# Ranks, rows and tables of the low nodes made under layer 1's first sums, and the plan for crowded nodes behind the last one-hot

## What is computed

```python
def _sage_conv(x, src, dst, Wl, Wr, b):
    agg = segment_sum(x[src], dst)            # 3125 rows
    deg = segment_sum(ones_like(dst), dst)
    mean = agg / maximum(deg, 1.0)[:, None]
    return mean @ Wl + x @ Wr + b
h = relu(conv1(h)); h = relu(conv2(h)); h = relu(conv3(h)); out = x + conv4(h)
```

## Time and profile before

| | |
|---|---|
| median of 3 runs | 645.88 us (645.56 to 646.54) |
| the profiled execution | 645.63 us, of it 643.8 us in the span of the trace |
| TensorE busy | 615.5 us (96%) |
| VectorE, ScalarE, GpSimd busy | 318.9, 194.1, 41.8 us |
| mean granted clock of TensorE | 0.986 of full speed |
| first fill, degrees, first round | TensorE's first step starts at 15.47 us, its degrees at 50.60, its first sum at 53.84; the degrees' last turn of the round at 103.29 |

### The profile page before, as it was taken

The page is one execution under the profiler, slowest core; times in us unless marked ns, Lnnn a source line. Parts: engine busy times, 40 slices in busy tenths (PEclk is TensorE's granted clock), DMA queues, the critical chain, the costliest instruction groups (busy, mean ns, idle before and its releaser), DMA issues.

```text
span 643.8 us, 10273 instructions
## 1 busy us (share of the span) xinstructions
PE 615.5 (96%) x4155; PEld 339.3 (53%) x4156; DVE 318.9 (50%) x616; ACT 194.1 (30%) x411; POOL 41.8 (6%) x91
## 2 busy tenths in 40 slices
PE   5678999999999999999999999999999999999998
PEld 4435555656555555554444445444445646556586
DVE  6977876878888779721211111111126343334421
ACT  3876866365653622300111001122122010000100
POOL 8001300000000000000000000000002020110110
PEclk9977999999999999999999999999999999999999
DMA  8401200510210202142433531534451133030330
GB/s 265 104 1 46 85 1 3 184 57 6 68 53 15 88 23 83 34 139 67 147 89 89 151 86 50 106 98 111 140 126 33 43 86 113 2 115 10 105 116 33
DMA packets 59687, 51.00 MB, mean 79 GB/s; under 512 B 31670, under 2 KB 44507, under 8 KB 59640
## 3 DMA queue, kind: packets, MB, share of 16 engines
q1 hardware_dynamic: 59284, 49.74, 26.8%
q0 software_dynamic: 240, 0.37, 0.2%
q10 hardware_dynamic: 116, 0.24, 0.1%
HBM read 28.15 MB, written 16.60 MB: 70 GB/s over the span
## 4 chain that ended last, share of the span: by engine, by line
PE 86%; DVE 6%; ACT 3%; DMA 2%; issue 2%; POOL 1%; SPq 0%; DVEq 0%; ACTq 0%; POOLq 0%
PE agg_ps L2362 34%; PE window_ps L2362 19%; PE lin_ps L2297 5%; PE window_ps L2183 5%; PE lin_ps L2246 3%; PE lin_ps L2140 2%; PE agg_ps L2338 2%; PE lin_ps L2266 2%; PE lin_ps L2305 2%; DVE early L1479 1%; PE lin_ps L2384 1%; PE degree_ps L2061 1%; PE turn_ps L2183 1%; PE window_ps L2338 1%; ACT counts L1876 1%
## 5 line engine op out<-in xcount | busy, mean ns | idle before, releaser
L2362 PE MATMUL agg_ps<-counts,H 128*128 128x512 f16 (+2 forms) x1026 | 235.1, 355 | 1.0 <-DVE aggT L1570 0.8
L2362 PEld LDWEIGHTS agg_ps<-counts,H 128*128 128x128 f16 (+1 forms) x1026 | 79.2, 98 | 56.2 <-issue 10.2
L1876 ACT ACTIVATE counts<-window_ps 128x400 f16<-128x400 f32 x150 | 73.5, 506 | 62.8 <-PE window_ps L2183 49.7
L1472 DVE TENSOR_TENSOR counts<-early 128x2048 f16<-128x2048 bf16 x66 | 78.0, 1213 | 7.2 <-PE window_ps L2183 4.8
L2362 PE MATMUL window_ps<-counts,early 128*128 128x512 f16 (+2 forms) x346 | 77.8, 379 | 0.0
L2362 PEld LDWEIGHTS window_ps<-counts,early 128*128 128x128 f16 (+1 forms) x346 | 33.5, 98 | 41.3 <-issue 3.4
L2362 PE MATMUL window_ps<-counts,H 128*128 128x512 f16 (+1 forms) x291 | 55.2, 346 | 0.0
L2183 PEld LDWEIGHTS window_ps<-counts 128*128 128x128 f16 x412 | 30.9, 99 | 33.2 <-issue 4.6
L1472 DVE TENSOR_TENSOR early<-early 128x1024 f16<-128x1024 bf16 (+1 forms) x69 | 43.9, 684 | 7.6 <-PE window_ps L2183 6.1
L2362 PE MATMUL agg_ps<-counts,early 128*128 (+4 forms) x297 | 46.5, 314 | 0.0
L2183 PE MATMUL window_ps<-counts 128*128 128x100 f16 x412 | 41.4, 210 | 1.0 <-DVE counts L1472 0.8
(11 more groups left out here) (302 smaller groups left out, 712.5 us busy)
## 6 DMA issues: line engine op xcount, KB each, us to landing
selfT<-hT_d SPq DMA_DIRECT2D x18, 512.0 KB, 4.2
hT_d<-newT SPq DMA_DIRECT2D x12, 512.0 KB, 4.6
rdeg<-rdeg_d SPq DMA_DIRECT2D x22, 256.0 KB, 4.1
counts<-in_x_dram SPq DMA_DIRECT2D x6, 512.0 KB, 8.1
hT_d<-counts SPq DMA_DIRECT2D x6, 512.0 KB, 3.6
newH<-in_x_dram SPq DMA_DIRECT2D x6, 512.0 KB
out_dram<-newT SPq DMA_DIRECT2D x5, 512.0 KB
hT_d<-newT SPq DMA_DIRECT2D x6, 256.0 KB, 3.8
```

What stands on the lines that cost most here:

```text
L1472: v.tensor_tensor(hots_of(group).rearrange("p r a (n d) -> p r a n d", d=2), pairs.unsqueeze(1).unsqueeze(1).broadcast_to([P, n, 2, P // 2 ...
L1876: a.activation(counts[:, :, 2 * w * WIN:2 * (w + 1) * WIN].rearrange("p t (a w) -> p a t w", a=2), window_bank(FILL_AT[w])[:, 0:2 * KEYS]. ...
L2362: last = m((agg_ps, window_ps)[bank][:, h, 0:n], tile[:, part, h * P:(h + 1) * P], counts[0:rows_, k, chunk_cols(c, n)], start=first and p ...
```

## The change

The diff leaves every operation as it is and moves some. On VectorE the four parts of `below` leave the fill and stand at sums 2, 3, 4 and 5 of the first round; `plan_high` moves from before pair 30 of the fill to behind its last pair; both `bases_late` go to sum 9, `late_rows` to 11, `square_weights` to 8, the tables to 16 and 20. On ScalarE three of the four moments of chunk place 4 leave the middle of the fill (one goes to its end), `first_rows(3)` goes from the fill's end to sum 8, the moments of places 5 and 6 and the norms move. On TensorE `rank_low` goes from pair 28 of the fill to sum 7, `own_products(1)` and `load_heavy` behind the last pair, `turn_bases` to sum 10, the squares to 10, 11 and 13, `select_late` to 14 and 18, now with waits for `norms_made` of 3 and `first_rows_made`. The squares wait for three tables instead of five; the wait for five stands at sum 24.

VectorE (`between` of the fill, then `first_round`):

```diff
-                       12: lambda: (below(0), h0_low_part(0)), 17: lambda: h0_low_part(1), 18: lambda: h0_shift(2),
-                       19: lambda: edge_tables(), 25: lambda: below(1), 28: lambda: (below(2), below(3)),
-                       30: lambda: plan_high()}
+                       12: lambda: h0_low_part(0), 17: lambda: h0_low_part(1), 18: lambda: h0_shift(2),
+                       19: lambda: edge_tables()}
...
+            plan_high()
             load_heavy(dve, regs, 0)
...
-            first_round = {0: lambda: (h0_moments(3), bases_late(2)), 1: lambda: (degrees(0), h0_low_part(2)),
-                           3: lambda: bases_late(3), 5: lambda: (late_rows(), h0_shift(3)), 7: lambda: h0_shift(4),
-                           9: lambda: h0_low_part(3), 10: lambda: square_weights(), 11: lambda: late_tables(2),
-                           12: lambda: h0_low_part(4), 13: lambda: h0_shift(5), 15: lambda: h0_low_part(5),
-                           16: lambda: (late_tables(3), h0_shift(6)), 21: lambda: h0_low_part(6)}
+            first_round = {0: lambda: h0_moments(3), 1: lambda: (degrees(0), h0_low_part(2)), 2: lambda: below(0),
+                           3: lambda: below(1), 4: lambda: below(2), 5: lambda: (h0_shift(3), below(3)),
+                           7: lambda: h0_shift(4), 8: lambda: square_weights(), 9: lambda: (bases_late(2), bases_late(3)),
+                           10: lambda: h0_low_part(3), 11: lambda: late_rows(), 12: lambda: h0_low_part(4),
+                           13: lambda: h0_shift(5), 15: lambda: h0_low_part(5), 16: lambda: late_tables(2),
+                           17: lambda: h0_shift(6), 20: lambda: late_tables(3), 21: lambda: h0_low_part(6)}
```

ScalarE (`between`):

```diff
-                       21: lambda: h0_moment(4, 0), 24: lambda: h0_moment(4, 1),
-                       25: lambda: (h0_copy(1), h0_moment(4, 2)),
-                       26: lambda: (h0_moment(4, 3), h0_high_part(2), own_copy(1)),
-                       31: lambda: (first_rows(3, slice(0, MID), degree_ps[:, 0:MID]), h0_moment(5, 0), h0_moment(5, 1))}
+                       21: lambda: h0_moment(4, 0), 25: lambda: h0_copy(1), 26: lambda: h0_high_part(2),
+                       31: lambda: (own_copy(1), h0_moment(4, 1))}
```

ScalarE, the new `first_round`:

```diff
+            first_round = {0: lambda: (h0_root(3), h0_moment(4, 2)), 1: lambda: h0_moment(4, 3),
+                           2: lambda: (h0_root(4), h0_moment(5, 0)), 3: lambda: h0_moment(5, 1),
+                           4: lambda: h0_moment(5, 2), 5: lambda: h0_copy(2),
+                           6: lambda: (h0_high_part(3), h0_moment(5, 3)), 7: lambda: own_copy(2),
+                           8: lambda: (first_rows(3, slice(0, MID), degree_ps[:, 0:MID]), h0_high_part(4), h0_copy(3)),
+                           9: lambda: h0_moment(6, 0), 10: lambda: h0_moment(6, 1),
+                           11: lambda: (h0_root(5), own_copy(3), norms(0)), 12: lambda: (h0_moment(6, 2), norms(1)),
+                           13: lambda: (h0_high_part(5), h0_moment(6, 3), norms(2)),
+                           14: lambda: (h0_root(6), late_sources(2)), 15: lambda: h0_copy(4),
+                           16: lambda: (own_copy(4), spread_sources(2)), 17: lambda: h0_high_part(6),
+                           18: lambda: late_sources(3), 21: lambda: spread_sources(3), 24: lambda: copy_degrees(0)}
```

TensorE (`squares`, `select_late`, the two tables, the fill's loop):

```diff
-                pe.wait_ge(step_tables, 5)
+                pe.wait_ge(step_tables, 3)
...
-                pe.wait_ge(lo_made, 3)
+                pe.wait_ge(first_rows_made, 1)
+                pe.wait_ge(norms_made, 3)
...
-                       27: lambda: h0_turn(1), 28: lambda: (rank_low(), own_products(1))}
-            first_round = {3: lambda: turn_bases(), 4: lambda: h0_turn(2), 7: lambda: own_products(2),
-                           8: lambda: (h0_turn(3), select_late(2)), 11: lambda: own_products(3),
-                           13: lambda: select_late(3), 15: lambda: h0_turn(4), 16: lambda: own_products(4),
-                           17: lambda: squares(0), 19: lambda: squares(1), 21: lambda: squares(2),
-                           24: lambda: turn_degrees(0)}
+                       27: lambda: h0_turn(1)}
+            first_round = {4: lambda: h0_turn(2), 7: lambda: (rank_low(), own_products(2)),
+                           8: lambda: h0_turn(3), 10: lambda: (turn_bases(), squares(0)),
+                           11: lambda: (own_products(3), squares(1)), 13: lambda: squares(2),
+                           14: lambda: select_late(2), 15: lambda: h0_turn(4), 16: lambda: own_products(4),
+                           18: lambda: select_late(3), 24: lambda: (pe.wait_ge(step_tables, 5), turn_degrees(0))}
...
-                if i == len(FILLS[-1]) - 2:
-                    load_heavy(pe, regs, 0)
...
+            own_products(1)
+            load_heavy(pe, regs, 0)
             heavy_of(-1)
```

More of the change, by code:

```diff
@@ L1982, in late_sources @@
                 whole_sources(piece + 1, p1 - p0, whole_late)
-            first_round = {0: lambda: h0_root(3), 1: lambda: h0_moment(5, 2),
-                           3: lambda: (h0_root(4), h0_moment(5, 3)), 5: lambda: h0_copy(2),
-                           6: lambda: h0_high_part(3), 7: lambda: (h0_moment(6, 0), h0_moment(6, 1), own_copy(2)),
-                           8: lambda: (h0_high_part(4), h0_copy(3)), 9: lambda: late_sources(2),
-                           10: lambda: h0_moment(6, 2), 11: lambda: (spread_sources(2), h0_root(5), own_copy(3)),
-                           12: lambda: h0_moment(6, 3), 13: lambda: (h0_high_part(5), h0_root(6)),
-                           14: lambda: late_sources(3), 15: lambda: h0_copy(4), 16: lambda: own_copy(4),
-                           17: lambda: (norms(0), h0_high_part(6)), 18: lambda: norms(1),
-                           20: lambda: spread_sources(3), 21: lambda: norms(2), 24: lambda: copy_degrees(0)}
+            first_round = {0: lambda: (h0_root(3), h0_moment(4, 2)), 1: lambda: h0_moment(4, 3),
[9 more added lines that the diff above has]
+                           18: lambda: late_sources(3), 21: lambda: spread_sources(3), 24: lambda: copy_degrees(0)}
             second_round = {0: lambda: h0_copy(5), 2: lambda: (root_row(0), h0_copy(6)),
```

## The result

| | before | after |
|---|---|---|
| median of 4 runs | 646.21 us (645.56 to 647.79) | 660.26 us (659.62 to 660.57) |
| the profiled execution, its span | 645.63, 643.8 us | 660.32, 658.5 us |
| TensorE's first step | 15.47 us | 16.11 us |
| degrees, first sum | 50.60, 53.84 us | 44.65, 48.06 us |
| last degree turn of the round | 103.29 us | 117.73 us |

The ratio is 1.022 (95% interval 1.0199 to 1.024). The predicted 649.1 us had the sign and not the size: the time lies 8 us above the range. All of the difference arises ahead of the last degree turn: it comes 14.4 us later, and the rest is unchanged. Of the 14.4 us, 0.64 arise before the fill: TensorE's first step starts later in this execution, where both kernels run the same code. The page of the changed kernel (busy time, then tenths in 40 slices of the span) shows where the rest is.

What follows compares the result with a forecast made beforehand. TensorE was taken to bound the first round, and VectorE and ScalarE the fill. Terms -7.2 + 3.45 + 1.0 + 1.0 + 4.15 + 1.25 - 0.2 = +3.45 on 645.63 gave 649.1 us, own range 647 to 651.4, 8-in-10 range 645.0 to 652.0.

Steps and rivals of the forecast that it cites:

- fill, from there to the degrees: Fill: without comparisons and ranks, ScalarE's copies and VectorE's plan let the degrees start near 43.4 us, -7.2 us.
- ranks: TensorE in the first round: sixteen rank products of 512 columns, covered by nothing, +3.45 us.
- sum 5: Sums 0 to 5: VectorE's degrees and comparisons delay one-hots that TensorE needs, +1.0 us (0 to 2).
- bases at sum 9: Sum 9: first rows behind the own copy, then bases, make one-hots late for TensorE, +1.0 us (0.5 to 1.5).
- squares and selection: Sums 11 to 14: three TensorE waits for norms that ScalarE reaches late, 1.95, 0.95 and 1.25, +4.15 us (2 to 5).
- tables at sum 20: Sum 20: late tables need sources selected at sum 18, so one-hots come late, +1.25 us (0 to 2).
- before's own short waits: Two short waits of the kernel before go with the moved turn_bases and selections, -0.2 us.
- The third rival: TensorE's clock falls in the new waits around sums 10 to 14, costing 2.8 us more: 651.9 us; chance 0.10.
- ScalarE's chain: Fill on ScalarE: 9.0 us of work after own_products(0) ends near 33.4, so the last window is stored at 42.6 us.
- The first rival: First round: TensorE stays the only bound, norms and tables come in time, 641.9 us; chance 0.14.
- the second: First round: the norms' 1.95 us is real, most other waits take each other's place, 645 us; chance 0.16.

Runs made afterwards that it cites:

- experiment 3: Changed kernel with the low parts of chunks 3 and 6 moved ahead of the bases and late tables on VectorE: 651.99 us, ratio 1.0101 to the kernel before.
- experiment 2: Changed kernel with only the low part of chunk 6 moved ahead of the late tables at sum 20 on VectorE: 657.26 us, ratio 1.0176 to the kernel before.
- experiment 5: Changed kernel with only the first rows moved ahead of the own copy of chunk 2 on ScalarE at sum 7: 655.01 us, ratio 1.0138 to the kernel before.
- experiments 1: Changed kernel with only the low part of chunk 3 moved ahead of the bases, at sum 9 on VectorE: 654.52 us, ratio 1.0133 to the kernel before.
- experiment 4: Changed kernel with both low parts moved up and each of three norms first in its place on ScalarE: 648.71 us, ratio 1.0045 to the kernel before.
- experiment 7: The version of experiment 4 with the low nodes' comparisons back in VectorE's fill, ranks still at sum 7: 651.92 us, ratio 1.0074 to the kernel before.
- experiments 9: Experiment 4 plus the fill's end rearranged, first rows ahead of own copy 2, late selection, sources and tables earlier: 645.62 us, ratio 0.9989 to the kernel before.
- 10: Experiment 9 plus later VectorE shift and high part of chunk 3, and ScalarE's own copy 3 one window copy later: 645.57 us, ratio 0.9993 to the kernel before.
- 6: Kernel before with only the plan for crowded nodes moved behind the last one-hot: 649.2 us, ratio 1.0043 to the kernel before.
- experiment 11: Experiment 9 with chunk 3's shift and high part as in experiment 10, heavy counts released ahead of the plan's end: 643.38 us, ratio 0.9963 to the kernel before.

## Why the prediction was right or wrong

| term | predicted | changed kernel | with both low parts moved (3) |
|---|---|---|---|
| start of TensorE's first step | none | +0.64 | +0.02 |
| fill, from there to the degrees | -7.2 | -6.59 | -6.59 |
| ranks | +3.45 | +3.46 | +3.46 |
| sum 5 | +1.0 | +1.28 | +1.28 |
| low part of chunk 3 at sum 8 | none | +5.11, clock +1.6 | 0 |
| bases at sum 9 | +1.0 | (hidden by the wait at 8) | +1.20 |
| squares and selection | +4.15 | 1.82 + 1.11 + 0.83 = +3.76 | +3.75 |
| a window copy at 104.65 | none | +0.74 | +0.74 |
| tables at sum 20 | +1.25 | (hidden by the wait there) | +1.22 + 0.47 |
| low part of chunk 6 at sum 20 | none | +2.88, clock +1.6 | 0 |
| before's own short waits | -0.2 | -0.5 | -0.3 |
| sum | +3.45 | +14.0 | +5.3 |
| last degree turn, by the traces | +3.5 | +14.4 | +6.0 |
| measured, by the medians | | +14.05 | +5.9 |

The terms of the two right columns are from the traces; the clock's are half of 3.2 us, the ranks' goes from their start to that of the next work. Of the 0.4 and 0.7 us that the sums lack, 0.2 lie in the degrees' products (3.41 us in place of 3.24); the rest is unexplained.

- *The sign and the frame were right.* TensorE has no slack in the round, so each wait there is paid; nothing changes behind it. Ranks, squares, and the waits near sums 5, 9 and 20 came within 0.4 us of their terms once the long waits were out (experiment 3).
- *The failed step is "Bases at sum 9, +1.0".* It asked only when TensorE wants the one-hots behind the bases, not what else stands behind them in VectorE's queue; the runs showed 5.11 us of wait there for the low part of chunk 3, a term that the sum put at nothing. I costed low parts as VectorE's time and never as something that TensorE waits for at sums 8 and 20, though `LOW_AT` is in the code. The same in "Tables at sum 20". Together 8 us of wait and 3.2 of clock, of which moving only the low parts gave 8.3 us back, since the smaller waits they hid then come out.
- *Clock.* The third rival (the clock falls in the new waits) happened, on top of the missed waits: 0.50 behind 5.11 us of idle time and a half-clock stretch behind 2.88 us, none behind 1.4 us and less (experiments 2 and 5). Its place was wrong: I gave it to the squares, whose waits of 1.8 and 1.1 us left it at 1.00. By the Trainium skill (TensorE: Matmul & The Clock Gate, "HAM oscillation — how this bites in real kernels") waits between bursts throttle again and again; the traces agree for the two waits of 5.1 us and for two of three of 2.88, and don't for the short ones. Its price wasn't fixed either: about 1.6 us each time in the changed kernel, 2.6 in experiment 2, nothing behind the 2.88 us of experiment 5. The 2.8 that I took from the fill's end lies just above these.
- *The fill was mis-sized by 0.6 us.* The degrees start at 44.65 us, where 43.4 was forecast, but 0.64 us of that is the late first step. From the first step to the degrees it took 35.13 us before and 28.54 in the changed kernel (28.54 to 28.70 in experiments 1 to 5, which share its fill). The plan's end was right: 26.87 us after the first step, against 42.2 - 15.47 = 26.7. From there to the degrees it took 1.67 us, where I took 1.23 and 0.77 from the earlier trace rows. In the kernel before neither stood behind a plan that had just ended: the plan was done at 43.92, TensorE had loaded ahead of its last two pairs, and VectorE's 1.23 us is put down to TensorE. So part of the load's time may have run beside other waits there; this is read from the trace, and no run tests it.
- *Two slips of adding changed little.* The terms of ScalarE's chain give 33.4 + 9.0 = 42.4, not 42.6, and those of the tables 3.75, not 3.85.
- *Squares: the size was right (3.76 of 4.15).* The expectation of experiment 4, that nothing covers the first norm, wasn't: with the norms first even the first wait goes.
- The first rival (TensorE stays the only bound) and the second (half the chain hides) fell: where a wait was hidden, a longer one hid it.

Left open: what decides whether, and for how long, the clock falls behind a wait of 2.88 or 5.1 us, and why the clock of experiment 7 differs from run to run. No version has comparisons in the fill together with the early release of the counts, and the kernel before wasn't run with that release. So it isn't shown that the moves themselves gain anything: without the release the best of them tie with the kernel before (experiments 9 and 10).

## What to carry to other kernels

When a step that waits for a far engine is moved in an in-order queue, price it by whoever waits for the entries behind it, not by its own consumer: list every semaphore that the bottleneck engine waits for and find the entry that raises it. Two neighbouring entries of a table swapped were worth 5.7 us of 660 here. A wait of several microseconds on TensorE can cost half clock as well (1.6 to 2.6 us here, once nothing), so a long one can be worth more than its length in short ones. Before a difference of under a microsecond between two profiles is put down to an edit, count from a common event ahead of it: the first step alone started between 15.09 and 16.16 us here. Where a wait goes to registers and branches, measure from the release to the next work, since the releaser named may be another that ended near it.

## What the runs showed that I had not expected

- In the changed kernel TensorE worked for some 3.2 us at 1.2 GHz after waits of 5.11 and 2.88 us, the second time only from a microsecond after its return. After 5.10 us in experiment 2 it was 5.3 us, and after 2.88 us in experiment 5 it stayed at 2.4 GHz, as it did after 1.82, 1.40 and 1.22 us.
- From the end of what the load waits for to the first degree product pass 1.67 to 1.68 us in the changed kernel and in every experiment but 6, whose load stands elsewhere.
- In every version the first sums behind the fill start at half clock. The degrees do so too in the changed kernel (0.50 from 44.6 to 48.1 us); in the kernel before they had 0.81 (50.6 to 53.8), in experiment 11, where TensorE idled 1.84 us ahead of them, 0.65 (41.2 to 44.6).
